# Attention scores on the four quarters of the PE array: 32-row contractions into four banks in a gated cross-attention and expert layer

## What is computed

```
h = layernorm(x)
Q = heads(h @ Wq.T + bq); K = heads(ctx @ Wk.T + bk); V = heads(ctx @ Wv.T + bv)   # 16 heads of 16
energy = einsum('bhqd,bhkd->bhqk', Q, K) / 4, masked keys at -1e10
x = x + tanh(g_xattn) * (softmax(energy) @ V @ Wfc.T + bfc)
n = layernorm(x); logits = n @ gate_kernel; the two largest of 8 experts, softmax of the two
x = x + tanh(g_ffn) * sum over the two: w * ((silu(n @ w0[e]) * (n @ w1[e])) @ wo[e])
```

## Time and profile before

| | us |
|---|---|
| median of 3 runs | 1432.3 |
| lowest, highest | 1430.13, 1432.6 |
| profiled execution | 1433.63 |
| its span, first to last instruction | 1432.1 |
| mean granted clock of TensorE | 0.979 of full |
| busy: PE, weight loads, DVE, ACT, POOL | 1336.5, 1170.9, 807.8, 695.3, 890.4 |

### The profile page before, as it was taken

The page is one execution under the profiler, slowest core; times in us unless marked ns, Lnnn a source line. Parts: engine busy times, 40 slices in busy tenths (PEclk is TensorE's granted clock), DMA queues, the critical chain, the costliest instruction groups (busy, mean ns, idle before and its releaser), DMA issues.

```text
span 1432.1 us, 35541 instructions
## 1 busy us (share of the span) xinstructions
PE 1336.5 (93%) x9634; PEld 1170.9 (82%) x9635; DVE 807.8 (56%) x2519; ACT 695.3 (49%) x1779; POOL 890.4 (62%) x1389
## 2 busy tenths in 40 slices
PE   3999999999999999999929999999999999999996
PEld 3898888888888888888828888888888888888885
DVE  3678878878878878878743333333333333333332
ACT  2566666666666666666623333333333333333332
POOL 3478888888888888888763444444444444444443
PEclk9999999999999999999969999999999999999998
DMA  5033323333223333223577884333333333333332
GB/s 149 18 112 110 109 74 109 122 125 109 96 83 111 118 124 114 91 81 118 180 226 201 207 219 106 57 53 53 55 53 54 55 52 55 51 55 51 55 56 34
DMA packets 73811, 139.70 MB, mean 98 GB/s; under 512 B 11568, under 2 KB 54992, under 8 KB 71600
## 3 DMA queue, kind: packets, MB, share of 16 engines
q0 software_dynamic: 32064, 52.46, 18.9%
q1 hardware_dynamic: 39696, 84.87, 18.3%
q10 hardware_dynamic: 2016, 1.93, 0.5%
HBM read 68.95 MB, written 70.27 MB: 97 GB/s over the span
## 4 chain that ended last, share of the span: by engine, by line
PE 54%; issue 12%; POOL 11%; DVE 11%; DMA 6%; ACT 5%; DVEq 1%; POOLq 1%; ACTq 0%; SPq 0%; another core or an unknown queue 0%
PE banks L1296 24%; PE psB L1315 12%; PE banks L1137 4%; DMA out_dram<-ey,eid 4%; PE psT L1304 4%; POOL routed_rows L478 3%; PE psG L1281 2%; PE psT L1149 2%; ACT prob L604 2%; ACT prob L608 2%; PE banks L1089 2%; DVE qT L809 2%; POOL rs L421 2%; PE banks L1133 1%; POOL rs L456 1%
## 5 line engine op out<-in xcount | busy, mean ns | idle before, releaser
L1296 PE MATMUL banks<-w_all,etT 128*128 x1620 | 433.2, 403 | 0.7 <-ACT etT L715 0.7
L1296 PEld LDWEIGHTS banks<-w_all,etT 128*128 128x128 f32 x1620 | 286.7, 189 | 51.1 <-issue 3.6
L1038 DVE TENSOR_TENSOR hgT<-psT,hgT 128x512 fp32r<-128x512 f32 x135 | 93.4, 692 | 414.4 <-ACT hgT L727 398.5
L531 POOL DMA_INDIRECT out_dram<-ey,eid x135 | 216.6, 1604 | 162.2 <-DMA out_dram<-ey,eid 46.8
L1315 PEld LDWEIGHTS psB<-w_all,hgT 128*128 128x128 f32 x1620 | 208.4, 188 | 18.4 <-issue 1.5
L526 POOL DMA_DIRECT2D et<-routed_rows x135 | 84.7, 627 | 223.0 <-issue 166.5
L1315 PE MATMUL psB<-w_all,hgT 128*128 x1620 | 217.7, 283 | 0.8 <-ACT hgT L727 0.8
L733 ACT ACTIVATE ey<-psB,ewt 128x256 f32<-128x256 f32 x135 | 64.1, 475 | 234.8 <-PE psB L1315 168.1
L721 ACT ACTIVATE hs<-banks 128x512 f32<-128x512 f32 x135 | 80.6, 597 | 185.1 <-PE psT L1304 179.3
L432 POOL TENSOR_TENSOR kbd<-kT,own 128x616 fp32r<-128x616 f32 x128 | 152.3, 1221 | 24.1 <-DVE kT L831 24.1
L1161 PE MATMUL psB<-vbd,probT 128*128 128x51 f32 x1280 | 158.1, 271 | 0.0
(11 more groups left out here) (159 smaller groups left out, 2305.2 us busy)
## 6 DMA issues: line engine op xcount, KB each, us to landing
split_weights<-w_part SPq DMA_DIRECT2D x16, 1536.0 KB
w_all<-split_weights SPq DMA_DIRECT2D x32, 768.0 KB
et<-routed_rows POOLq DMA_DIRECT2D x135, 129.0 KB
xb<-in_x_dram SPq DMA_DIRECT2D x32, 256.0 KB, 2.8
w_raw<-in_L_ffn_w_kernel_dram SPq DMA_DIRECT2D x32, 256.0 KB
out_dram<-x SPq DMA_DIRECT2D x64, 128.0 KB
w_raw<-in_L_ffn_wo_kernel_dram SPq DMA_DIRECT2D x16, 256.0 KB
cb<-in_ctx_dram SPq DMA_DIRECT2D x32, 77.0 KB
```

The costliest lines, as they stand in the source:

```text
L531: gp.indirect_dma_start(out=out, out_offset=bass.IndirectOffsetOnAxis(ap=eid[:, u:u + 1], axis=0), in_=ey[:, u % 2, :], in_offset=None, co ...
L1038: dve.tensor_tensor(hgT[:, 1].rearrange("p c q -> p (c q)"), psT[:], hgT[:, 0].rearrange("p c q -> p (c q)").bitcast(F32), ALU.subtract).t ...
L1296: m = pe.matmul(banks4[:, bank], etT[:, u % 2, a, c], weight(e, c, w, n), start=(j == 0), stop=(j == len(steps) - 1))
```

## The change

The array's rows are used in four groups of 32. A contraction over 32 partitions covers two heads, so a key block is spread over two heads only (kbd has HP = 2 heads a chunk in place of 8, and POOL writes it in two instructions a batch of 2 x 2 x 77 columns). Row group j writes bank j, four heads a bank (two of each chunk), all of banks4. A block of scores is four mask matmuls of 308 columns and 24 matmuls of 154 columns, in the order part, chunk, row group. For this the output rows of Wq and Wk and their biases are permuted: ACT copies the transposed weights of these two in two pieces with another order, and the biases come in 16 loads of 32 words on SP's queue, behind the load of the gate kernel, in place of four loads of 128 words on ACT's.

As all four banks of banks4 now hold scores, psK, the logits (psL) and the ranks (psR) move to psB, and psY to psG. The orders of work and the waits follow: PE's `gate` waits for this tile's o_norm (o_sb), stands ahead of `project`, and `rank` stands between them; `values` stands ahead of gate; n2_T stands ahead of the last attend group and waits for oT_sb; ctx_T and keys wait for o_sb and l_cp in place of x1_done. On DVE the reduction of the last four heads and negate come first; free_rows moves behind o_norm, and the copy of the logits moves from ACT to DVE (`logits`). s_ps is raised by the last matmul of each row group, so four times for a tile. The core of the diff:

```
-    HB = 512 // K2
+    ROWS = 32
+    HP = ROWS // HD
+    RG = P // ROWS
+    HB = HP * DC
+    S_BANKS = [(n, h, HB) for n, h in enumerate(range(0, H, HB))]
+    S_FULL = RG - 1
+    PAIR = HP * K2
+    assert len(S_BANKS) == RG == 4 and HB * K2 <= 512
...
-        kbd = sb("kbd", [P, 2, 2, DC, HC, K2], F32R)
+        kbd = sb("kbd", [P, 2, 2, DC, HP, K2], F32R)
+        own2 = sb("own2", [P, HP])
...
-        psS, psK, psY = banks4[:, 0:3], banks4[:, 3], banks4[:, 3, D:2 * D]
+        psS = banks4
+        psK, psL, psR = psB[:, H * VW:H * VW + DC * K2], psB[:, 440:440 + E], psB[:, 448:448 + 2 * E]
+        psY = psG[:, D:2 * D]
...
+            with nc.allow_non_contiguous_dma(reason="biases, one word a partition"):
+                for n, v in enumerate((bk, bq)):
+                    for c in range(DC):
+                        for j in range(RG):
+                            h = (j * DC + c) * ROWS
+                            sp.dma_start(bias[j * ROWS:(j + 1) * ROWS, 1 - n, c:c + 1], v[h:h + ROWS].rearrange("(q o) -> q o", o=1)).then_inc(const_in, 16)
...
-                for a, c in ((a, c) for a in range(2) for c in range(DC)):
-                    gp.tensor_tensor(kbd[:, u, a, c], kT2[:, a, c].bitcast(F32).rearrange("p (o k) -> p o k", o=1).to_broadcast([P, HC, K2]),
-                                     own[:].rearrange("p (h o) -> p h o", o=1).to_broadcast([P, HC, K2]), ALU.mult).then_inc(kbd_done, 1)
+                for a in range(2):
+                    gp.tensor_tensor(kbd[:, u, a], kT2[:, a].bitcast(F32).rearrange("p c (o k) -> p c o k", o=1).to_broadcast([P, DC, HP, K2]),
+                                     own2[:].rearrange("p (o s l) -> p o s l", o=1, l=1).to_broadcast([P, DC, HP, K2]), ALU.mult).then_inc(kbd_done, 1)
...
+                if name in ("wk", "wq"):
+                    for c in range(DC):
+                        m = act.copy(wT[name][:, c].rearrange("p (c j q) -> p j c q", c=DC, j=RG),
+                                     banks4[:, n, c * D:(c + 1) * D].rearrange("p (j c q) -> p j c q", c=DC, j=RG))
...
-
-            def l_evac(i):
-                act.wait_ge(g_ps, i + 1)
-                if known(i, 1):
-                    act.wait_ge(l_idx, i)
-                act.copy(logit[:], psG[:, D:D + E]).then_inc(l_cp, 1)
...
-            dve.memset(share[:], 1.0 / P).then_inc(valid_done, 1)
+            dve.memset(share[:], 1.0 / ROWS).then_inc(valid_done, 1)
...
             dve.wait_ge(valid_done, 17)
...
-                dve.wait_ge(s_ps, i + 1)
+                dve.wait_ge(s_ps, RG * (i + 1))
...
+                dve.wait_ge(s_max, 2 * i + 1)
+                dve.tensor_scalar(neg_mx[:, t], mx[:, t, S_FULL * HB:H], -scale, None, ALU.mult).then_inc(s_neg, 1)
+
+            def s_shift(i, t):
                 dve.wait_ge(s_max, 2 * (i + 1))
-                dve.tensor_scalar(neg_mx[:, t], mx[:, t, S_FULL * HB:H], -scale, None, ALU.mult).then_inc(s_neg, 1)
-
-            def s_shift(i, t):
...
+            def logits(i):
+                dve.wait_ge(g_ps, i + 1)
+                if known(i, 1):
+                    dve.wait_ge(l_idx, i)
+                dve.tensor_copy(logit[:], psL).then_inc(l_cp, 1)
...
-                    dve.tensor_tensor(pos[:], psG[:, D + E:D + 2 * E], base[:], ALU.add).then_inc(pos_done, 1)
+                    dve.tensor_tensor(pos[:], psR[:, 0:E], base[:], ALU.add).then_inc(pos_done, 1)
...
-                        s_largest(i + 1, 1 - t, 0)
+                        s_largest(i + 1, 1 - t, 1)
                     if keys:
                         k_split(b + 1, 0)
-                    if placed:
-                        free_rows(i - 3, 0)
-                    if softmax:
-                        s_largest(i + 1, 1 - t, 1)
-                    if keys:
-                        k_split(b + 1, 1)
-                    if placed:
-                        free_rows(i - 3, 1)
                     if t == 1 and more:
                         v_split(b + 1, 1)
                     if softmax:
                         s_negate(i + 1, 1 - t)
+                        s_largest(i + 1, 1 - t, 0)
+                    if keys:
+                        k_split(b + 1, 1)
                     if t == 1 and more:
                         v_split(b + 1, 2)
                     if softmax:
                     o_norm(i)
                     if t == 1 and more:
                         v_evac(b + 1, 1 - u)
+                    if placed:
+                        free_rows(i - 3, 0)
+                        free_rows(i - 3, 1)
+                    if known(i, 2):
+                        logits(i - 2)
                     if known(i, 1):
                         residual_1(i - 1, u if t else 1 - u, 1 - t, b if t else b - 1)
-                    if known(i, 3):
+                    if placed:
                         place(i - 3, (u4 - 3) % 4)
                     if known(i, 2):
                         choose(i - 2)
...
-                pe.wait_ge(kbd_done, 2 * DC * (b + 1))
+                pe.wait_ge(kbd_done, 2 * (b + 1))
                 pe.wait_ge(mrow_done, b + 1)
                 if known(i, 1):
                     pe.wait_ge(s_sub, i)
-                    pe.wait_ge(s_heads, (H - S_FULL * HB) * i)
-                for n, h, k in S_BANKS:
-                    pe.matmul(psS[:, n, 0:k * K2], share[:], mrow[:, u].rearrange("p (o k) -> p o k", o=1).to_broadcast([P, k, K2]),
+                    pe.wait_ge(s_heads, HB * i)
+                for j in range(RG):
+                    r0 = j * ROWS
+                    pe.matmul(psS[:, j, 0:HB * K2], share[r0:r0 + ROWS], mrow[r0:r0 + ROWS, u].rearrange("p (o k) -> p o k", o=1).to_broadcast([ROWS, HB, K2]),
                               start=True, stop=False, skip_group_check=True)
-                for (q_part, k_part), (n, c, h0, h1) in ((part, piece) for part in PARTS for piece in S_PIECES):
-                    first = S_BANKS[n][1]
-                    m = pe.matmul(psS[:, n, (h0 - first) * K2:(h1 - first) * K2], qT[:, u, q_part, c, t * P:(t + 1) * P],
-                                  kbd[:, u, k_part, c, h0 - c * HC:h1 - c * HC].rearrange("p h k -> p (h k)"),
-                                  start=False, stop=True, skip_group_check=True)
-                m.then_inc(s_ps, 1)
+                for q_part, k_part in PARTS:
+                    for c in range(DC):
+                        for j in range(RG):
+                            r0 = j * ROWS
+                            m = pe.matmul(psS[:, j, c * PAIR:(c + 1) * PAIR], qT[r0:r0 + ROWS, u, q_part, c, t * P:(t + 1) * P],
+                                          kbd[r0:r0 + ROWS, u, k_part, c].rearrange("p h k -> p (h k)"),
+                                          start=False, stop=True, skip_group_check=True)
+                            if (q_part, k_part) == PARTS[-1] and c == DC - 1:
+                                m.then_inc(s_ps, 1)
...
             def project(i):
                 pe.wait_ge(oT_sb, DC * (i + 1))
+                if known(i, 1):
+                    pe.wait_ge(n2T_sb, i)
...
             def n2_T(i, u4):
                 pe.wait_ge(xn2_done, i + 1)
-                if known(i, 1):
-                    pe.wait_ge(base_done, i)
+                if below(i, NT - 1):
+                    pe.wait_ge(oT_sb, DC * (i + 2))
+                else:
+                    pe.wait_ge(x1_done, NT)
...
             def gate(i):
                 pe.wait_ge(n2T_sb, i + 1)
                 for c in range(DC):
-                    m = pe.matmul(psG[:, D:D + E], xn2T[:, c], gate_sb[:, c], start=(c == 0), stop=(c == DC - 1))
+                    m = pe.matmul(psL, xn2T[:, c], gate_sb[:, c], start=(c == 0), stop=(c == DC - 1))
...
                     prob_T(i, t, 1)
                     if t == 0 and more:
                         queries(b + 1, 0)
-                    if t == 0:
-                        if more:
-                            pe.wait_ge(k_raw, DC * (b + 2))
-                    elif more2:
-                        pe.wait_ge(ctxT_sb, b + 3)
                     if known(i, 1):
                         o_T(i - 1)
-                    if known(i, 3):
-                        rank(i - 3)
                     if t == 0 and more:
                         queries(b + 1, 1)
+                        pe.wait_ge(k_raw, DC * (b + 2))
+                    if t == 1 and more2:
+                        pe.wait_ge(ctxT_sb, b + 3)
                     attend(i, u, b, 0)
                     prob_T(i, t, 2)
                     attend(i, u, b, 1)
-                    attend(i, u, b, 2)
                     if known(i, 2):
                         n2_T(i - 2, (u4 - 2) % 4)
+                    attend(i, u, b, 2)
+                    if t == 0 and more:
+                        values(b + 1)
                     if t == 1 and more:
                         flatten_values(b + 1)
+                    if known(i, 2):
+                        pe.wait_ge(o_sb, i + 1)
```

(42 more changed lines are left out.)

18 lines of the change are left out of this document (8 added, 10 removed).

## The result

The changed kernel takes 1444.2 us (median of 4 runs, 1443.1 to 1446.8) against 1432.5 us beside it: ratio 1.0091, 95% interval 1.0074 to 1.0109. It is slower by 0.9%, where 1416 was forecast and faster given 0.60. Its profiled execution took 1446.8 us, span 1444.9.

A forecast was written before the change was run, and what follows sets the result against it. PE was taken as the bound, with DVE close behind. A gain of 0.6 us a batch over 30 batches, 18 us, less 2 for setup, gave 1417.6 profiled, 1416 against the median; range 1385 to 1463.

The forecast's parts named there:

- The score block: Masks and score matmuls on PE: 1.25 us a tile against 2.37 before, if row groups load and stream together.
- The round of four: Four score matmuls, one per row group, working together: 0.106 us a round, six rounds 0.65 us.
- emptying the array: Draining PE's array at both ends of the score block: 0 to 0.2 us each, 0.2 taken each.
- The rival of loads one after another: Score block's weight loads run serially: block 2.75 to 3.15 us, kernel 1443 to 1463 us; chance 0.27.
- The loop of DVE: DVE's chain through one attention batch, new waits included: 20.7 or 21.3 us, 21.0 taken, against 21.6 before.
- X to residual: DVE, from the end of o_norm at t=0 through PE's gate, rank and project to the residual: 1.86 us.
- The halves of the batch: Between ends of o_norm on DVE: 9.12 us from t=0 to t=1, then 11.56 or 12.16 to the next t=0.
- The second rival: New waits in the attention stage eat the gain: 21.5 to 21.7 us a batch, 1430 to 1438 us; chance 0.10.
- The clock: Attention stage: PE idles 1.5 us before gate at t=1; its work was still priced at full clock.
- something else slower: Rival of another slowdown, as the granted clock falling to its lower level where PE now idles; chance 0.05.
- The setup: Before the attention stage: 16 tiny bias loads on SP's queue delay ScalarE by 0 to 9 us, 2 taken.
- POOL: Four kbd instructions of 1.22 us become two of half that: 3.6 us a batch less, worth nothing more.

The follow-up runs named there:

- e2_fill: Changed kernel plus three throwaway bf16 matmuls ahead of values or flatten_values and three ahead of the wait before gate: 1407.2 us, ratio 0.9807.
- e11_before_wait: Kernel before the change plus one wait, PE waiting for this tile's o_norm ahead of project: 1478.3 us, ratio 1.0292.
- e6_gatefree_exp: Changed kernel with gate and rank in psT's bank, gate not waiting for o_norm, and exp_gap moved behind n2_evac and exp_scores: 1386.9 us, ratio 0.9639.
- e10_fill1: Changed kernel plus one throwaway matmul ahead of values or flatten_values and one ahead of the wait before gate: 1412.3 us, ratio 0.9836.

## Why the prediction was wrong

The time, 1444.2, lies in the range of 1385 to 1463, but on the other side of "before". By steps:

- **The score block: right in kind, too dear.** 1.25 us was the sum, 0.87 was measured. The round of four is 0.11 us as counted: 24 matmuls last 0.90 us and one 0.27, which leaves 0.63 for the other 23, 0.027 each. What was mis-sized are the masks, 0.19 us counted and 0.04 from their start to that of the first score matmul, and the 0.4 us for emptying the array, for which under 0.2 is left in 0.87. The rival of loads one after another (0.27) is refuted by the block's 0.87 us. The Trainium skill's page "TensorEngine Tiling (Array Packing)", section "Key Properties", has tiles that load and multiply in parallel, and the trace agrees. The Trainium skill's page "TensorE: Matmul & The Clock Gate", section "LDWEIGHTS (loading the stationary operand)", gives a 32-row load the time of a full one; the trace agrees with that as well (0.187 us recorded for one in e2_fill, 0.190 in the kernel before), but it doesn't speak against the change, since four of them go at once.
- **The loop of DVE: right, with some luck in the sum.** Middle 21.0 us a batch at full clock, measured 21.03 in e2_fill. X to residual 1.86, measured 1.73 in the piece above. The halves of the batch in e2_fill, between the ends of o_norm from 250 to 450 us, are 8.79 us in the mean, where 9.12 was counted, and 12.25, where 11.56 or 12.16 was: two errors that cancel. The second rival, that the waits eat the gain, did not happen by the loop.
- **The clock: the step that failed.** The prediction wrote "PE idles before `gate` instead", 1.5 us at t=1, and priced PE's work at full clock all the same. It saw one pause a batch; the trace has four, of 0.4 to 0.7 us at full clock in the batch shown, 2.4 us together. The fall of the clock stood among the rivals as "something else slower", with 0.05. It should have been asked of every pause that the change moves to PE. A pause where PE is not late costs nothing by the chain of waits; here the clock fell behind such pauses, and 24% of the stretch of 200 us ran at the lower level. In the sum the missing term is 41 us (2.8%), against 28 us gained at full clock.
- **The evidence for it was at hand.** The clock row of the page had its one fall between start and end in the changeover, where PE pauses. In the attention stage before, PE was busy 190 of 200 us, and the single edit of e11_before_wait brings it to 187 and the clock to 0.94. How far from such a fall the kernel before stood could not be read from its trace; that it could fall could. The Trainium skill's page "TensorE: Matmul & The Clock Gate", section "A second HAM failure mode: psum-queue depth-cycling", tells of a kernel in which frequent short idles of PE between groups of matmuls make the clock swing between its two levels; the trace after agrees, with swings behind pauses of PE of 0.9 us at most between 250 and 450 us, and it was not weighed in the prediction.
- **The setup: too dear.** 2 us were taken off, bounds 0 to 9. The 16 loads were issued from 7.5 to 17.3 us, at 0.42 to 0.49 us each in the median and one of 2.2, and landed after 4.6 us (keys) and 2.6 us (queries) in the median; ScalarE's first norm activation (xn) started at 19.10 us, as early as before (19.29).
- **POOL.** kbd instructions of half the size take 0.70 us, not 0.61; nothing waits for them.

## What to carry to other kernels

A change that takes work from TensorE and puts waits in its place can lower its clock, and then its work gets dearer for as long as the clock is down; read the granted clock beside each pause, and count a term for it whenever PE stops being the last to arrive. When a profile shows such a fall, throwaway matmuls into a free bank in the pauses are a quick test (37 us here) and, if the pauses can't go, a remedy; take the waits away first, and look where they go: e6_gatefree_exp, without a filler and at 0.90 of the clock, is as fast as the best version with fillers. Contractions of 32 rows on the four quarters paid here: 0.87 us against 2.37 for the same scores, in fp32r, provided that four banks are there to be written.

## What the runs showed of the hardware that was not expected

- In the changed kernel, with pauses of PE of 0.4 to 0.9 us, two a tile, the granted clock was 0.88 instead of 1.00, with PE still busy 181 of 200 us.
- The share of time in which PE is busy doesn't tell the clock: 179 of 200 us went with 0.98 in e10_fill1, 187 with 0.94 in e11_before_wait and with 0.90 in e6_gatefree_exp.
- Added work that is thrown away made the kernel faster: 1.2 us a tile, 37 us off the whole (e2_fill).
- Four weight loads of 32 x 128 in f32, each recorded with 0.19 us, and their matmuls go in a round of 0.11 us on four row groups.
